# Layer 1's softmax in six pieces, and layer 2's sum in one pass, in a four-layer graph network kernel

## The reference

```python
# layer 1: attention over neighbours, 8 heads of 16 features
g_l = (h @ W_l.T).reshape(b, n, H, F); g_r = (h @ W_r.T).reshape(b, n, H, F)
g_sum = g_r[:, :, None] + g_l[:, None]
e = einsum('bijhf,f->bijh', leaky_relu(g_sum, 0.2), w_attn)
e = where(mask == 0, -inf, e * mask)
a = softmax(e, axis=2)
out = leaky_relu(einsum('bijh,bjhf->bihf', a, g_r).reshape(b, n, H*F), 0.2)

# layer 2: an MLP on each pair of nodes, normalised, summed with the adjacency
h = relu(hi[:, :, None] + hj[:, None] + b1)
y = layernorm(h @ W2 + b2) * gamma + beta
out = einsum('bij,bijh->bih', adj, y)
```

## Time and profile before

| what | value |
|---|---|
| median of 3 runs | 1713.37 us (1710.48 to 1713.9) |
| the profiled execution's own time | 1708.26 us |
| its span, first to last instruction | 1706.5 us |
| mean granted TensorE clock | 0.95 of 2.4 GHz |
| PE busy | 86% of the span |
| DVE busy | 70% |
| ACT busy | 56% |
| DMA over the span | 366.82 MB, mean 215 GB/s |

### The profile page before, as it was taken

The page is one execution under the profiler, slowest core; times in us unless marked ns, Lnnn a source line. Parts: engine busy times, 40 slices in busy tenths (PEclk is TensorE's granted clock), DMA queues, the critical chain, the costliest instruction groups (busy, mean ns, idle before and its releaser), DMA issues. The chain is left out here.

```text
span 1706.5 us, 32127 instructions
## 1 busy us (share of the span) xinstructions
PE 1460.6 (86%) x9657; PEld 1247.2 (73%) x9721; DVE 1196.0 (70%) x2322; ACT 959.0 (56%) x2535; POOL 5.4 (0%) x24
## 2 busy tenths in 40 slices
PE   3664788989899898998989975999999999998564
PEld 3553556868787677877868774899999999997554
DVE  4886677677777777677777644566666666666788
ACT  2564786656556565565655312566666666665554
POOL 0000000000000000000000000000000000000000
PEclk9997899999999999999999997999999999999877
DMA  2220567868668676776767655867667667671122
GB/s 69 75 62 14 214 253 283 302 237 289 246 259 300 225 275 244 275 295 227 276 245 277 253 183 195 315 236 254 252 235 256 247 238 255 245 248 46 56 75 68
DMA packets 137523, 366.82 MB, mean 215 GB/s; under 512 B 12896, under 2 KB 71904, under 8 KB 137440
## 3 DMA queue, kind: packets, MB, share of 16 engines
q1 hardware_dynamic: 137040, 365.81, 59.7%
q10 hardware_dynamic: 400, 0.00, 0.0%
HBM read 231.54 MB, written 134.22 MB: 214 GB/s over the span
## 5 line engine op out<-in xcount | busy, mean ns | idle before, releaser
L863 DVE TENSOR_TENSOR b_wt<-bank,b_aT 128x512 f32<-128x512 f32 (+1 forms) x192 | 109.5, 599 | 142.3 <-PE bank L703 140.2
L1153 DVE TENSOR_REDUCE c_var<-c_ysq 128x4 f32<-128x512 f32 (+1 forms) x192 | 114.1, 594 | 117.0 <-ACT c_ysq L1101 95.7
L661 PE MATMUL wide<-b_vv,put_w 128*128 128x512 f32 (+1 forms) x384 | 171.8, 529 | 24.5 <-DVE b_vv L838 22.6
L1043 PE MATMUL wide<-W2c,c_h 128*128 128x128 f32 x1280 | 174.4, 275 | 4.5 <-issue 0.2
L838 DVE TENSOR_TENSOR b_vv<-bank,b_vv 128x512 f32<-128x512 f32 (+1 forms) x192 | 114.3, 599 | 86.9 <-ACT b_vv L759 83.7
L1043 PEld LDWEIGHTS wide<-W2c,c_h 128*128 128x128 f32 x1280 | 170.0, 193 | 4.3
L687 PE MATMUL bank<-b_wt,b_SITl 128*128 128x136 f32 x1280 | 162.8, 283 | 7.4 <-DVE b_wt L863 7.4
L687 PEld LDWEIGHTS bank<-b_wt,b_SITl 128*128 128x128 f32 x1280 | 158.7, 192 | 14.0 <-DVE b_wt L863 9.4
L703 PE MATMUL bank<-b_grl,b_SJl 128*128 128x128 f32 x1280 | 154.6, 276 | 5.1 <-ACT b_os L786 3.4
L1073 PEld LDWEIGHTS bank<-c_z,c_SIT 128*128 128x128 f32 x1280 | 153.9, 193 | 5.5 <-DVE c_z L1161 2.3
L1073 PE MATMUL bank<-c_z,c_SIT 128*128 128x128 f32 x1280 | 154.5, 276 | 2.1 <-DVE c_z L1161 2.1
(11 more groups left out here) (213 smaller groups left out, 2949.8 us busy)
## 6 DMA issues: line engine op xcount, KB each, us to landing
si_d<-b_SI SPq DMA_DIRECT2D x64, 640.0 KB, 3.0
sj_d<-b_SJ SPq DMA_DIRECT2D x64, 640.0 KB, 4.0
sit_d<-b_SIT SPq DMA_DIRECT2D x64, 640.0 KB, 5.0
b_SJl<-sj_d SPq DMA_DIRECT2D x64, 640.0 KB, 5.3
b_SITl<-sit_d SPq DMA_DIRECT2D x64, 640.0 KB, 5.7
c_SJ<-sj_d SPq DMA_DIRECT2D x64, 640.0 KB, 4.0
c_SI<-si_d SPq DMA_DIRECT2D x64, 640.0 KB, 5.2
c_SIT<-sit_d SPq DMA_DIRECT2D x64, 640.0 KB, 4.2
```

The lines of the kernel that those rows point to most:

```text
L661: pe.matmul(out, e.put_w[:, pos, :], vv[:, (pos + k) % 2, 0:width(k)], start=(pos == 0), stop=False)
L863: v.tensor_tensor(wt[:, mb, 4 * k:4 * k + rr, 0:P].rearrange("p r (h f) -> p r h f", h=HEADS), ring[k][:, 0:P * rr].rearrange("p (r h f) - ...
L1043: d = pe.matmul(bY[k][:, a:a + P], h[:, k, a:a + P], e.W2c[:, :], start=False, stop=(j == last))
L1153: v.tensor_reduce(var[:, k, 0:r], ysq[:, k, 0:width(k)].rearrange("p (j f) -> p j f", f=P), AX.X, ALU.add).then_inc(sum_ok, 1)
```

## The change

1. `every_step` has no loop any more: every step of layers 1 and 2 is written out.
2. Layer 1: LAG is 14. The six DVE pieces stand in positions 0 to 5, one in each, between `bend(1)` and the weighting of S. The exponential is in position 5 (from 2), T in position 6 (from 3). `finished` is moved to positions 3 and 7, the residual (`joined`) to 0 and 4, `centre` alone to 1 and 5. The exponential and the four squares of `centred` now meet on ACT in position 5, in that order, ahead of `evacuate_rows`.
3. Layer 2: `SIT` is fp32r. `z` is split into a high part (ACT, `keep_high`, three casts per graph) and a low part (DVE, `keep_low`, three subtractions), both in `zz` (fp32r, 128x256 per tile), and one matmul per tile multiplies `SIT` with both. The two sums stand side by side in a double bank `duo`; per four graphs ACT copies the low sums (`rest`) and DVE adds them. The pipeline of the projections starts one step earlier, the sum comes two steps behind the gather (one before), and the work is ordered by chunk: chunk 2 of graph n - 1 is squared, totalled and scaled in step n. The gather uses two banks in turn, in place of three.

```diff
-def every_step(eng, step, extra, first=1):
-    step(0, -1, False)
-    for n in range(8 * first):
-        step(n // 8, n % 8, False)
-    with eng.Fori(first, B // 8 - 1) as K:
-        for pos in range(8):
-            step(K, pos, True)
-    for n in range(B - 8, B + extra):
+def every_step(eng, step, extra, early=1):
+    for n in range(-early, B + extra):
         step(n // 8, n % 8, False)
...
-        LAG = 11
+        LAG = 14
...
                         bend(1)
+                    if soft(n, 0):
...
+                        z.add(v.tensor_tensor(mark[:, 1:ECAP], es[H:2 * H, 1:ECAP], es[H:2 * H, 0:ECAP - 1], ALU.subtract))
+                    if soft(n, 1):
...
+                        forward(0, LOWEST)
+                    if soft(n, 2):
...
+                        forward(HALF, top[:, HALF - 1:HALF])
+                    if soft(n, 3):
...
+                        backward(HALF, LOWEST)
+                    if soft(n, 4):
...
+                        backward(0, top[:, HALF:HALF + 1])
+                    if soft(n, 5):
...
+                        v.tensor_tensor(top[:, :], es[0:H, :], top[:, :], ALU.subtract).then_inc(z_ok, 1)
                     if S:
...
-        s.SIT = sb("SIT", [P, 4, TILES, P])
+        s.SIT = sb("SIT", [P, 4, TILES, P], F32R)
+        zz = sb("zz", [P, 2, TILES, 2 * P], F32R)
...
-                            d = pe.matmul(bO[:, a:a + P], s.SIT[:, (pos - 1) % 4, j, :], z[:, (pos - 1) % 2, j, :],
+                            d = pe.matmul(bO[:, r, :, :], s.SIT[:, r, j, :], zz[:, pos % 2, j, :],
...
+                    def keep_high(n, b, k):
+                        act.wait_ge(z_ok, 3 * n + k + 1)
...
+                        act.copy(zz[:, b, tiles(k).start:tiles(k).stop, 0:P],
+                                 z[:, b, tiles(k).start:tiles(k).stop, :]).then_inc(zh_ok, 1)
...
+                    def keep_low(n, b, k):
+                        js = slice(tiles(k).start, tiles(k).stop)
+                        v.wait_ge(zh_ok, 3 * n + k + 1)
+                        v.tensor_tensor(zz[:, b, js, P:2 * P], z[:, b, js, :], zz[:, b, js, 0:P].bitcast(F32),
+                                        ALU.subtract).then_inc(zl_ok, 1)
```

More of the change, by code:

```diff
@@ L566, in summed, with soft, finished, joined @@
             return inner or LAG < n <= B + LAG
[L568 to L584, removed]
+        def soft(n, k):
+            return n % R == k and R <= n <= B + k
+        def finished(n):
+            return n % Q == 3 and n >= LAG + 5
+        def joined(n):
+            return n % Q == 0 and n >= LAG + 6
+        def centred(n):
+            return n % Q == 1 and n >= LAG + 7
+        def fours(n):
+            return (n - LAG - 5) // Q
+        def eights(m):
+            return m // R + 1
         def pair_bank(pos, k):
@@ L865, in step @@
                                             att.unsqueeze(3).broadcast_to([P, rr, HEADS, HF]), ALU.mult).then_inc(w_ok, 1)
-                    if finished(n, pos, inner):
-                        part = os[:, (pos // Q) % 2, :, :]
-                        f = Steps(v, seq_c, 7 * fours(K, pos))
+                    if finished(n):
+                        part = os[:, fours(n) % 2, :, :]
+                        f = Steps(v, seq_c, 7 * fours(n))
                         v.wait_ge(os_ok, n - LAG - 1)
@@ L1076, in step @@
                     if A:
+                        mlp(0)
+                    if N2:
+                        pe.wait_ge(xT_ok, n + 3)
+                        pe.matmul(bP[:, P:3 * P], xT[:, :], e.W1s[:, :, :], start=True, stop=True).then_inc(p_mm, 1)
+                    if A:
+                        gather(n, pos, 2)
+                        mlp(1)
+                    if N:
+                        pe.wait_ge(lo_ok, g + 1)
+                        pe.wait_ge(sj_in[(pos + 1) % 4], rounds(K, pos + 1))
+                        pe.wait_ge(si_in[(pos + 1) % 4], rounds(K, pos + 1))
+                        gather(g, pos + 1, 0)
+                    if A:
                         mlp(2)
-                every_step(pe, step, 7)
+                every_step(pe, step, 7, 2)
             @block.scalar
@@ new lines, in step @@
+                    if N2:
+                        act.wait_ge(p_mm, n + 3)
+                        if inner or n >= 2:
+                            act.wait_ge(s.u_mm, 3 * n - 3)
+                        act.copy(hi[:, (pos + 2) % 4, :], bP[:, P:3 * P]).then_inc(hi_ok, 1)
+                    if F:
+                        keep_high(n - 1, (pos - 1) % 2, 2)
+                    if A:
+                        rectify(n, pos, 2)
+                        root(n, 0)
+                    if part(n, pos, inner, 1):
+                        act.wait_ge(o_mm, n - 1)
+                        if inner or n > Q + 1:
+                            act.wait_ge(o_read, batches(K, pos) - 1)
+                        act.copy(rest[:, :, :], bO[:, :, 1, :]).then_inc(rest_ok, 1)
@@ L1218, in step @@
                     if A:
-                        total(2)
-                        scale(2)
-                every_step(v, step, 7)
+                        scale(n, pos % 2, 1)
+                every_step(v, step, 7, 2)
 class Masks:
@@ L1873, in adjacency_stack @@
         general = sb("general", [P, 1], I32)
-        banks = [pb(f"bank{i}", [P, 512]) for i in range(5)]
+        banks = [pb(f"bank{i}", [P, 512]) for i in range(3)]
+        duo = pb("duo", [P, 2 * 512])
+        banks += [duo[:, 512 * i:512 * (i + 1)] for i in range(2)]
         wide = pb("wide", [P, 3 * 512])
@@ L2045, in adjacency_stack @@
         e.wide = wide
+        e.duo = duo
         e.banks = banks
```

278 lines of the change are left out of this document (141 added, 137 removed).

## The result

| | before | after |
|---|---|---|
| median of 4 runs each, same chip | 1713.15 us (1710.48 to 1713.9) | 1642.68 us (1639.47 to 1644.35) |
| the profiled execution | 1708.26 us | 1644.35 us |
| its span | 1706.5 us | 1642.6 us |

A forecast was written before the change was run, and what follows sets the result against it. PE was taken to bound layer 2, and layer 1's ordinary steps kept PE busy, with 12.9 us lost per softmax. 1708.3 - 47 (layer 1) - 25 (layer 2) = 1636 us, as a median 1641; range 1598 to 1682.

The forecast's parts named there:

- the first S later: Layer 1's start: three more steps have no S, 8.05 us each, less 1.7 for three steps disturbed before: +22.5 us.
- from the first S to the S of the first step without a gather: Layer 1: steps with both halves of the work fall from 53 to 50, 678 us to 606: 72 us less.
- from there to the last S: Layer 1's end: three more steps with S and O alone, +16.8 us; waits of last softmax and centring gone, -14.
- The six pieces cost nothing: Layer 1: pieces fit DVE's 1.89 us idle time, five of six cost nothing; position 0 0.2 us late, position 2 0.3.
- The new meeting on ACT: Layer 1, position 5: exponential and squares delay the evacuations, PE loses about 3.0 us; excess per eight steps 4.3, not 12.9.
- PE: Layer 2: ten one-pass sum matmuls take 1.2 us where the sum took 2.23; PE's step is 6.9 us, 1.03 less.
- DVE: Layer 2: DVE works 7.03 us a step and becomes the bound; with 0.25 and 0.2 us of waits, 7.5 a step.
- The ends: Layer 2: a pipeline one step longer at its end takes 2 us off the 27 us gain.
- The second one: Layer 2: nearly each DVE operation starts only when the one before ended; no gain there, 1666 us; chance 0.20.
- The first rival: Everything fits: DVE waits for nothing in layer 2, evacuations disturb T little, 2 us less per softmax; 1599 us; chance 0.17.
- The third and the fourth: Layer 1's pieces not covered or fetch competes: 1678 us, chance 0.08; layer 2's handing to and fro sets step: 1775, 0.05.
- Written-out steps costed at nothing: Layers 1 and 2: fetching more code costs nothing; a saved loop turn is worth a few tenths at most, none counted.

The follow-up runs named there:

- the first and the third of the three edits: Changed kernel with the softmax's exponential earlier on ACT: 1617.74 us; changed kernel with PE's second gather ahead of its waits for T's input: 1619.39 us.
- the two counter-tests: Changed kernel with layer 2's normalise_x ahead of rest and squares on ACT: 1640.3 us; changed kernel with two layer 2 DVE operations on POOL: 1632.37 us.
- the two edits of ACT's order: Changed kernel with exponential earlier and squares one position later, measured together with two DVE operations moved to POOL: 1594.18 us, ratio 0.9312.
- e2_layer1_alone: Layer 1's change alone, layer 2 and its loop as in the kernel before: 1666.17 us, ratio 0.9739 of before.
- e6_pool_parts: Changed kernel with two of layer 2's DVE operations per four graphs moved to POOL: 1632.37 us, ratio 0.9538 of before.
- e7_order_alone: Changed kernel with layer 2's sum kept in float32, without high and low parts, new order kept: 1659.47 us, ratio 0.969 of before.
- e9_x_first: Changed kernel with layer 2's normalise_x on ACT ahead of the copy of rest and the squares: 1640.3 us, ratio 0.9587 of before.

## Why the prediction was right, and where its terms were off

The median of 1642.68 us is 1.7 us above the forecast of 1641. The mechanisms were right, but that the figure is so close is luck. Inside the sum a step left out of a reading, 8 us of gain, stands against softmax steps priced too low, 11 us of loss (both below). And the sum as a whole promised 72 us, where the profiled executions differ by 63.9 and the medians by 70.5. It was made for an execution like the profiled one, which stood 5 us below its median: 1636 us. The profiled execution of after took 1644.35: 8 us more, and it stood 1.7 above its median. So 6.7 of the 8 us fall away between executions of the same kernels, which no term of the sum foresaw.

**Layer 1** (-47 forecast, -43.1 measured):

| term | forecast | measured |
|---|---|---|
| the first S later | +22.5 | +21.9 |
| from the first S to the S of the first step without a gather | 606 us in place of 678, -72 | 616.7 in place of 686.3, -69.6 |
| from there to the last S | +16.8 - 14 = +2.8 | 73.4 in place of 68.2, +5.2 |
| behind the last S | 0 | -0.6 |

- *The 678 us of before* were read one step short. Its last gather starts at 962.25, so the S of the first step without a gather is the one at 966.77:

```profile
958.92 2.39 PE L703 MATMUL bank<-b_grl,b_SJl 128*128 128x128 f32 x20
...
962.25 0.27 PE L430 MATMUL bank<-b_SJ,b_hi 128*128 128x256 f32 x1
...
966.77 1.39 PE L703 MATMUL bank<-b_grl,b_SJl 128*128 128x128 f32 x11
```

From the first S at 280.49 that is 686.3 us for 53 steps; the 678 end at 958.92 and are 52. With 686 the sum would have had 8 us more gain, 55 in place of 47, and 1633 us as the forecast. The 8 us offset most of the mis-sized term below.
- *The six pieces cost nothing*: right. Every ordinary step is 11.5 us, and one in eight 11.7 (forecast 0.3 more in position 2). 0.59 us are idle behind the piece where the forecast said less than 0.4.
- *The new meeting on ACT*: right in its place and its cause, with 2.67 us of waiting for 3.0. **This is the term that was mis-sized**: "Per eight steps the excess is 3.0 + 0.8 + 0.5 = 4.3 us". The step with T measured 18.2 - 11.5 = 6.7 over an ordinary one, and eight steps 99 us for 97.1. T itself was taken as 0.83 us, from a row at full clock, but the pause that I had forecast is nearly always followed by 1.2 GHz, which makes the work behind it 2.8 us longer. The step of 15.4 us with the same pause at full clock shows it, and so do the first and the third of the three edits. The kernel before had a hint: the clock of its windows around a softmax is below 1.

Two windows of before around PE's two waits of 1.76 us in a softmax (they end at 451.87 and 468.64), which I had not weighed (PEclk is the sixth entry behind the length):

```profile
451.00:458.00 7.00, 6.13 (x36) 5.51 (x37) 5.01 (x9) 2.54 (x5) 0.00 (x0) 0.76 0.43 175
460.00:474.00 14.00, 10.61 (x54) 7.93 (x54) 12.11 (x20) 6.88 (x20) 0.00 (x0) 0.88 0.48 174
```

- Six softmaxes at 2.4 us more are 14.4 us; the ordinary steps gave back 50 x 0.07 = 3.5: 606 + 14.4 - 3.5 = 616.9, for 616.7 measured. (The first of the 50 has 2.8 us more, behind the first softmax, and the last 3.5 less, since the next gather is missing; both were left out and nearly cancel.)
- *Drain*: 2.4 us worse than forecast. The S that waited 15.3 us follows its neighbour by 7.1 now, where 5.9 was taken; the rest was not followed up.

**Layer 2** (-25 forecast, -22.0 measured):

- *PE*: the sum is 1.03 us shorter, as forecast. The first steps, in which DVE has no parts yet, run at 6.9 us, the PE's forecast step.
- *DVE*: busy 0.906 x 7.61 = 6.9 us a step, forecast 7.03. The one wait per step that I had found for the cast is there (46 times in 350 us, 16.5 us in total, 0.36 each):

```profile
DVE c_zz L1208 <- ACT c_zz L1130: 16.5, 46, 0.4
DVE c_var L1191 <- ACT c_ysq L1119: 8.9, 22, 0.5
```

The wait costs 0.36, not 0.25, and the second row is a wait that I had not found, 0.2 us per step. The step is 7.61 us, forecast 7.5. That DVE is the bound is shown by the two counter-tests (the order of ACT changes nothing, work taken off DVE does).
- *The ends*: the forecast's -2 us was met, but as a difference and in part by luck: the new pipeline is 10.7 us faster over its first four steps (21.9 for 32.6 us) and 13.1 us slower behind the last transpose (44.2 for 31.1). In the other kernels with the new layer 2 and its one-pass sum those four steps vary from 19.4 to 22.7 us.

**Rivals.** The second one, by which each DVE operation costs its whole duration, would have layer 2 unchanged; it gained 22.0 us, and a sum that stands behind a scaling starts 0.61 us after it, as the two rows below show. By the rule of the Trainium skill ("VectorE: DVE Perf Modes", The DRAIN you can't avoid) as I had weighed it they would be 0.69 apart. The same section adds that a next operation that is not held starts earlier, and the trace agrees with that. The code has two semaphore waits between the two operations (L1188, L1190), so a wait that is already met does not cost the 0.08 us on which this rival rested:

```profile
1236.56 0.69 DVE L1201 TENSOR_TENSOR c_z<-wide,c_var 128x512 f32<-128x512 f32 x1
1237.17 0.41 DVE L1191 TENSOR_REDUCE c_var<-c_ysq 128x2 f32<-128x256 f32 x1
```

The first rival had the excess of a softmax 2 us lower, 2.3 us; with the two edits of ACT's order it is 12.8 - 11.5 = 1.3 us. So a kernel that fast was two small edits away. The third and the fourth left no trace: the pieces are covered, and layer 2's step is far from 8.6 us.

**Written-out steps costed at nothing**: this step was wrong too, they bring a gain. In the kernel before it is worth 6 to 11 us. The forecast of this part said "a few tenths at most" for a turn; the turn in layer 2 measures 0.3 us, and the rest is small shortenings of many steps. The Trainium skill ("Runtime: NRT & Kernel Launch", Instruction fetch mechanics) says that code is fetched ahead in sequence and that a taken branch whose target is not at hand stalls for the fetch. The run agrees in sign, with 0.3 us a turn in layer 2; whether the fetch or the loop's own instructions take them was not tried.

## What to carry to other kernels

When a term of a sum says that PE will idle for some microseconds, look up the granted clock behind the nearest such pause and price the work behind it at that clock: here the pause cost 2.7 us and the clock another 2.8, in 27 of 30 such steps. An engine's wait names who came last, not who sets the pace: move the supposed cause and see whether the mean of a whole period changes; that of layer 2's four steps did not. A count of steps is worth checking against where the work really ends: one step too few gave this forecast 8 us. And work that meets on a side engine once in eight steps (here an exponential and four squares on ACT, 62% busy) can be worth an edit of a few lines: 22 to 29 us for each of the three here.

## What was not expected of the hardware

- The same pause at the same place is not always followed by the same clock. In the changed kernel and the four others with this pause (`e2_layer1_alone`, `e6_pool_parts`, `e7_order_alone`, `e9_x_first`), leaving out each one's first softmax, 27 of 30 pauses of 2.67 us are followed by some 6.4 us at a granted clock of 0.50 and a step of 18.1 to 18.4 us. Behind two the low stretch is shorter (17.0 and 17.1 us), behind one there is none (15.4). Pauses of 1.06, 1.52 and 1.76 us were followed by a low clock in none, one and one of six steps. In the kernel before both waits of 1.76 us in the softmax above were, and ahead of the second PE had idled another 1.63 us shortly before. So the length of the pause alone does not decide it; what else does was not tried.
- A POOL operation slows DVE's subtraction of two SBUF tensors: 1.17 us in each of the 15 meetings in layer 2, 0.69 us alone. DVE operations with one operand in PSUM or a single operand showed no change beside it (scaling 0.69; `total` 0.68 and, for 256 columns, 0.41). The DVE operation ends 0.55 us behind the POOL one each time, nearly its own full length, as if it had waited. The Trainium skill ("SBUF — State Buffer", Who interferes with whom) says that the pair of ports that the two engines share is an exclusive lock, that a VectorE instruction with two inputs in SBUF contends for it with a GpSimd one that reads SBUF, and that one with at most one SBUF input does not, certain performance modes aside. The rows agree.
- POOL takes 1.04 us for a 128x512 multiplication of float32 where DVE takes 0.69, and it paid all the same: POOL was idle, and the kernel became 10 us shorter.
